# Eight-head attention layers: q and k in two rounded-fp32 parts, 48 rows per head, two heads in the two 64-row halves of the array

## The reference

```python
h = group_norm(x, 32 groups) * gn_w + gn_b
qkv = einsum('oc,bct->bot', qkv_w, h) + qkv_b          # 3 x 128 rows
q, k, v = split of qkv.reshape(B * 8, 3 * 16, T)
w = softmax(einsum('bct,bcs->bts', q * scale, k * scale))   # 1024 x 1024 per head
a = einsum('bts,bcs->bct', w, v)
x = x + einsum('oc,bot->bct', proj_w, a) + proj_b
```

## Time and profile before

| | |
|---|---|
| median of 3 runs | 2327.98 us (2327.2 to 2330.86) |
| profiled execution: span, first to last instruction | 2324.5 us |
| what lies around the span (median less span) | 3.5 us |
| TensorE busy / weight loads busy | 2210.8 us (95%) / 974.3 us |
| DVE busy / ACT busy / POOL busy | 1817.7 us / 1720.3 us / 520.4 us |
| mean granted TensorE clock | 0.987 |

### The profile page before, as it was taken

One profiled execution on the slowest core, in us unless ns is written; L12 is line 12 of the kernel. 1 busy time (PEld: TensorE's weight loads), 2 busy tenths in 40 slices (PEclk: granted clock), 3 DMA queues, 4 the chain that ended last, 5 costly groups with the idle time before them and its releaser, 6 DMA issues. The chain is left out here.

```text
span 2324.5 us, 34217 instructions
## 1 busy us (share of the span) xinstructions
PE 2210.8 (95%) x11776; PEld 974.3 (42%) x11776; DVE 1817.7 (78%) x3176; ACT 1720.3 (74%) x3107; POOL 520.4 (22%) x689
## 2 busy tenths in 40 slices
PE   3999999999999999999999999999998999999998
PEld 1223232323332232333233232323325888888887
DVE  2878878878887887888788878888846777777776
ACT  1467777767866776777777777777777888888887
POOL 3113030302213030212113030212003333333331
PEclk9999999999999999999999999999998999999999
DMA  8053361606243361616154251606102121121111
GB/s 153 10 66 58 52 79 44 94 20 91 44 65 60 51 89 25 100 26 88 34 77 62 47 79 33 105 22 91 25 16 75 43 67 57 42 66 57 42 52 48
DMA packets 81935, 136.86 MB, mean 59 GB/s; under 512 B 17760, under 2 KB 50656, under 8 KB 81632
## 3 DMA queue, kind: packets, MB, share of 16 engines
q1 hardware_dynamic: 78496, 133.90, 32.4%
q10 hardware_dynamic: 3264, 0.79, 0.2%
HBM read 57.31 MB, written 22.02 MB: 34 GB/s over the span
## 5 line engine op out<-in xcount | busy, mean ns | idle before, releaser
L450 DVE TENSOR_REDUCE h_half_nmax<-h_s_ps 128x1 f32<-128x512 f32 x2048 | 1286.8, 685 | 299.3 <-PE h_s_ps L689 292.3
L603 ACT ACTIVATE h_probs<-h_st_ps 128x512 f32<-128x512 f32 x2048 | 1104.2, 599 | 417.3 <-PE h_st_ps L826 411.4
L826 PE MATMUL h_st_ps<-h_qrep,h_krep 99*128 99x512 bf16 x2048 | 784.0, 384 | 54.1 <-issue 24.9
L689 PE MATMUL h_s_ps<-h_krep,h_qrep 96*128 96x512 bf16 x2048 | 799.6, 391 | 22.4 <-SPq L232 20.9
L681 PE MATMUL h_pv<-h_probs,h_vT 128*32 128x512 f32 x4096 | 552.0, 611 | 0.9 <-ACT h_probs L603 0.7
L689 PEld LDWEIGHTS h_s_ps<-h_krep,h_qrep 96*128 96x128 bf16 x2048 | 200.5, 98 | 682.4 <-DVE h_half_nmax L450 500.7
L826 PEld LDWEIGHTS h_st_ps<-h_qrep,h_krep 99*128 99x128 bf16 x2048 | 202.6, 99 | 251.5 <-issue 56.2
L1343 PE MATMUL o_s<-o_k,o_q 128*128 128x512 f32 x768 | 225.1, 429 | 7.4 <-DVE o_q L1164 5.7
L348 POOL TENSOR_SCALAR h_nparts<-h_nmax 128x16 bf16<-128x16 f32 x64 | 16.4, 256 | 956.0 <-DVE h_nmax L458 956.0
L1343 PE MATMUL o_pv<-o_pT,o_vT 128*128 128x512 f32 x768 | 207.3, 406 | 0.8 <-ACTq L1270 0.8
L1158 DVE TENSOR_TENSOR o_pT<-o_t,o_pT 128x512 fp32r<-128x512 f32 x256 | 164.6, 685 | 45.6 <-ACT o_pT L1295 43.1
(11 more groups left out here) (116 smaller groups left out, 1381.3 us busy)
## 6 DMA issues: line engine op xcount, KB each, us to landing
h_krep<-h_kp SPq DMA_DIRECT2D x96, 256.0 KB, 8.6
h_qrep<-h_qp SPq DMA_DIRECT2D x192, 128.0 KB, 9.5
x_res<-out_dram SPq DMA_DIRECT2D x32, 512.0 KB, 3.4
num<-av SPq DMA_DIRECT2D x128, 64.0 KB
rrep<-rden_dram SPq DMA_DIRECT2D x16, 512.0 KB
out_dram<-o_y SPq DMA_DIRECT2D x16, 512.0 KB
h_x_in<-out_dram SPq DMA_DIRECT2D x15, 512.0 KB, 3.4
out_dram<-h_y SPq DMA_DIRECT2D x15, 512.0 KB, 2.7
```

Of the source, the lines that this page charges most:

```text
L450: reduce = nc.vector.tensor_reduce(half_nmax[:, c, unit:unit + 1], s_ps[bank(2 * n + c)][:, :], AX.X, ALU.max, negate=True)
L603: nc.scalar.activation(probs[g % 2][:, j, :], st_ps[bank(n)][:, :], ACT.Exp, scale=1.0 / CH ** 0.5).then_inc(exp_done, 1)
L689: nc.tensor.matmul(s_ps[bank(n)][:, :], qrep[par][0:KS, th, head, tile * P:(tile + 1) * P], krep[par][0:KS, head, c * HALF:(c + 1) * HALF] ...
L826: nc.tensor.matmul(st_ps[bank(n)][:, :], krep[par][0:KM, head, st * P:(st + 1) * P], qrep[par][0:KM, th, head, :], start=True, stop=True). ...
```

## The change

q and k are split into two fp32r parts (a rounded one and what is left), and three products are kept: 3 x 16 = 48 rows of contraction per head, 51 with the maxima. Head 2m goes to rows 0 to 63 and head 2m+1 to rows 64 to 127, and their matmuls stand next to each other in TensorE's order. The maxima stay in three bf16 parts but travel as fp32r, in two DMAs. The rows of ones are filled at the start, before the coefficients, and `replicate` waits for them. TensorE's order in a group becomes st0, st1, s0, s1, st2, st3, products(k-1), s2, s3, shared bank.

```diff
-TERMS = 6
+TERMS = 3
+ROWS = P // 2
 KS = TERMS * CH
-KM = KS + 3
+MAX_PARTS = 3
+KM = KS + MAX_PARTS
...
-        qrep = [sb(f"qrep{i}", [P, 2, HEADS, HALF], BF16) for i in range(2)]
-        krep = [sb(f"krep{i}", [P, HEADS, T], BF16) for i in range(2)]
+        qrep = [sb(f"qrep{i}", [P, 2, HEADS // 2, HALF], F32R) for i in range(2)]
+        krep = [sb(f"krep{i}", [P, HEADS // 2, T], F32R) for i in range(2)]
...
         def split_parts(engine, own, which):
-            own.mark(tt(middle, whole, lead, ALU.subtract))
-            own.done(tt(rest[:, :], whole, lead, ALU.subtract))
-            own.done(tt(last, rest[:, :], middle, ALU.subtract))
+            own.done(engine.tensor_tensor(parts[which][:, 1, :], full[which][:, :], parts[which][:, 0, :].bitcast(F32),
+                                          ALU.subtract))
...
             def replicate(par, u):
-                for term, part in enumerate((0, 1, 2, 0, 1, 0)):
-                    sp.dma_start(krep[par][term * CH:(term + 1) * CH, :, :], parts["k"][:, part, :]).then_inc(rep_dma, 16)
+                for term, part in enumerate((0, 0, 1)):
+                    for r in range(2):
+                        to, of = r * ROWS + term * CH, slice(r * ROWS, (r + 1) * ROWS)
+                        sp.dma_start(krep[par][to:to + CH, :, :].bitcast(F32),
+                                     parts["k"][of, part, :].bitcast(F32)).then_inc(rep_dma, 16)
...
+                for term, part in enumerate((0, 1, 0)):
+                    for r in range(2):
+                        for th in range(2):
+                            sp.dma_start(qrep[par][to:to + CH, th, :, :].bitcast(F32), ...
...
+            sp.wait_ge(ones, 1)
             replicate(0, 0)
...
             pool.wait_ge(consts, CONSTS)
+            for par in range(2):
+                for r in range(2):
+                    own.done(nc.gpsimd.memset(krep[par][r * ROWS + 32:(r + 1) * ROWS, :, :].bitcast(F32), 1.0))
+            pool.sem_inc(ones, 1)
...
             def send_max_rows(step, th):
-                act.dma_start(qrep[par][KS:KM, th, quad * QUAD:(quad + 1) * QUAD, :],
-                              mrow[th][:, :]).then_inc(mrow_dma, 16)
+                for r in range(2):
+                    act.dma_start(qrep[par][r * ROWS + KS:r * ROWS + KM, th, quad * 2:(quad + 1) * 2, :].bitcast(F32),
+                                  mrow[th][r * MAX_PARTS * MP:(r + 1) * MAX_PARTS * MP, :].bitcast(F32)).then_inc(mrow_dma, 16)
...
+                    def scores_ahead(k, c):
+                        for r in range(2):
+                            n = STEP * s + 4 * k + 2 * c + r
+                            pe.wait_ge(max_done, last_in_bank(n) + 1 + 4)
+                            row_scores(n, ms // 2 % 2, ms % 2, pair, c, r)
+
+                    def column_scores(k, m):
+                        for r in range(2):
+                            n = QUAD * (GROUPS * s + k) + 2 * m + r
+                            rows = slice(r * ROWS, r * ROWS + KM)
+                            pe.wait_ge(exp_done, last_in_bank(n) + 1 + QUAD)
+                            nc.tensor.matmul(st_ps[bank(n)][:, :], krep[par][rows, quad * 2 + m, st * P:(st + 1) * P],
+                                             qrep[par][rows, th, quad * 2 + m, :],
+                                             start=True, stop=True).then_inc(st_ready, 1)
...
                     for k in range(GROUPS):
+                        column_scores(k, 0)
+                        scores_ahead(k, 0)
+                        column_scores(k, 1)
+                        if not (first and s == 0 and k == 0):
+                            products(k - 1)
+                        scores_ahead(k, 1)
+                        in_shared_bank(k)
```

More of the change, by code:

```diff
@@ L105, in many_heads @@
     MH = UNITS // 2
+    MP = MH // 2
     LEAD = 12
@@ L476, in _ @@
             dve.sem_inc(misc_for_dve, -3)
-            for unit in range(2 * LEAD):
-                maximum(unit - 2 * LEAD, unit, 2 * LEAD)
+            for pair in range(LEAD):
+                for c in range(2):
+                    maximum(4 * (pair - LEAD) + 2 * c, pair, c, 4 * LEAD)
             dve.sem_inc(scores_ready, -4 * LEAD)
@@ L505, in body @@
                                 output(base + 4, 0, no_output)
-                        for unit in (2 * k, 2 * k + 1):
-                            if s % 2 == 1 and unit % 2 == 1 and STATS <= k < STATS + 4 and not (last and s == 3):
+                        for c in range(2):
+                            if s % 2 == 1 and c == 1 and STATS <= k < STATS + 4 and not (last and s == 3):
                                 if k == STATS:
@@ L684, in group_products, with row_scores @@
                 return product
[L686 to L690, removed]
+            def row_scores(n, par, quad, pair, c, r):
+                th, m, tile = pair // MP, quad * 2 + pair % MP // (TILES // 2), pair % (TILES // 2)
+                rows = slice(r * ROWS, r * ROWS + KS)
+                nc.tensor.matmul(s_ps[bank(n)][:, :], qrep[par][rows, th, m, tile * P:(tile + 1) * P],
+                                 krep[par][rows, m, c * HALF:(c + 1) * HALF],
                                  start=True, stop=True).then_inc(scores_ready, 1)
@@ L805, in in_shared_bank @@
                                 project_output(1)
-                    def m_unit(unit, half):
-                        of_next, m = divmod(unit + 2 * LEAD, UNITS)
+                    def scores_ahead(k, c):
+                        of_next, pair = divmod(k + LEAD, GROUPS)
                         ms = s + of_next
@@ L811, in m_unit @@
                             return
-                        n = STEP * s + 2 * unit + half
-                        pe.wait_ge(max_done, last_in_bank(n) + 1 + 4)
-                        if m == 0 and half == 0 and ms % 2 == 0:
+                        if pair == 0 and c == 0 and ms % 2 == 0:
                             pe.wait_ge(rep_ready, u + 1)
-                        row_scores(n, ms // 2 % 2, ms % 2, m, half)
-                    for k in range(GROUPS):
[L819 to L828, removed]
-                            if j == 2 and not (first and n < QUAD):
-                                products(k - 1)
-                            m_unit(2 * k + j // 2, j % 2)
-                            if j == 3:
-                                in_shared_bank(k)
```

78 lines of the change are left out of this document (41 added, 37 removed).

## The result

The changed kernel takes 2505.98 us (median of 4 runs, 2493.26 to 2514.55), the kernel before 2327.59 us beside it. The ratio is 1.0765 (95% interval 1.0724 to 1.0806): 178 us slower. Slower was forecast, at 2387 us and with 2480 as the upper end, so the measured time lies above the range.

What follows compares the result with a forecast made beforehand. TensorE's stream bounded the eight-head layers, 2.84 us per plain group; after the change, bank waits would, at 2.86. 16 x (3.7 + 2.1 - 1.7) = +66, -7 at the start, gave 2387 us (+59), range 2300 to 2480.

Steps and rivals of the forecast that it cites:

- TensorE's stream was the bound: Eight-head layers before the change: scores follow one another without waits, 2.84 us per plain group, DVE's floor 0.4 below.
- a pair streams in the time of one: Scores of two heads in the two row halves: a pair takes 0.23 us, four pairs 0.92 instead of 1.75.
- The waits for banks become the chain.: Plain groups in the new order: s2, its reduction, s1, st3, products with three banks; 2.86 us per group, +0.02.
- Exposed four-byte loads, 0.16 a group.: Weight loads at s2 and s1 that cannot hide: 0.08 us each, twice in the chain, 2.70 becoming 2.86.
- Shared-bank groups, +0.4 and +0.2.: Groups with a projection: k and q 4.10 us against 3.70, values and output 3.93; four of each per image.
- Two DMAs for the maxima, +2.1.: Two issues in a row hold ACT 1.5 us before exp1: +2.1 us per image, bounds 0 and 3.0.
- Replicate shorter in four-byte elements.: Copying of k and q: same bytes in four-byte elements land sooner, q ending near 964 instead of 977.
- The stall at the step's start: Wait for the maxima's send behind the replicate, group 5.40 instead of 3.7 us: it goes, -1.7 us per image.
- Start, -7.: Before the first row score: ones delay coefficients 8.5 us, shorter split and DMAs save more; 45.6 against 53.1 us.
- rival (d): A TensorE idling a third of the time stays at 1.2 GHz: groups about 1.4 us longer, near 3000 us; chance 0.05.

Runs made afterwards that it cites:

- e3_same_half: The changed kernel with every score matmul in rows 0 to 63, odd heads left out and even ones computed twice: 3858.08 us, ratio 1.658.
- e1_order: The changed kernel with TensorE's old order within a group, halves, types and DMAs as changed: 2365.01 us, ratio 1.0179.
- e2_bf16: The changed kernel with two parts, maxima rows and replicas in bf16, third part of q and k left out: 2334.69 us, ratio 1.0031.
- e7_spread: The changed kernel with the maxima's two DMAs apart, the first behind exp0, the second behind exp2: 2581.43 us.
- e9_all: e5_hold_late with the column scores over all 64 rows of a half, as in e6_rows64: 2280.32 us, ratio 0.9799.
- e10_all_spread: e9_all with the maxima's two DMAs apart, as in e7_spread: 2252.84 us, ratio 0.9689.
- e5_hold_late: e1_order with q's second-half DMAs held until the next step's maxima rows land, and ones filled after the coefficients: 2330.11 us, ratio 0.9979.
- e8_before_48rows: The kernel before with bf16 score matmuls over 48 rows instead of 96 and 99, and a smaller exponential scale: 3715.24 us (one run).
- e6_rows64: The changed kernel with column scores over all 64 rows of a half, the added 13 rows zeros against ones: 2457.84 us, ratio 1.0569.
- e4_twice: The changed kernel with st0 and st1 issued twice into the same bank: 2550.26 us, ratio 1.0967.

## Why the prediction was wrong

The direction and the chain were right, the size was not: +178 us instead of +59. By its own steps:

- **TensorE's stream was the bound, and a pair streams in the time of one.** Right: both matmuls of a pair in 0.50; without the pairing a group is 1 us longer at the lower level (e3_same_half).
- **"The waits for banks become the chain."** Right, and shown twice: the timeline has each step of it, and the order alone (e1_order) brings 2.94 to 2.70 and the time down by 141 us. The size was forecast as 2.86: 0.10 instead of 0.08 for an exposed load, twice, and 0.04 in the rest. Over 17 plain groups that is 1.4 us per image.
- **Exposed four-byte loads, 0.16 a group.** Right in kind; e2_bf16 measures 0.23 with the shorter steps of bf16 in it. The Trainium skill ("TensorE: Matmul & The Clock Gate", "Weight-path perf modes — Fast Weight Load (FWL) and DoubleRow") gives Fast Weight Load no win for fp32. The traces agree for fp32r: 195 ns a load in the changed kernel, 94 in e2_bf16.
- **Shared-bank groups, +0.4 and +0.2.** Mis-sized: k and q groups are 4.24 (+0.54, forecast 4.10), values 4.11 to 4.18 (+0.4, forecast 3.93). Groups 13 and 14 of a first step, which hold the output projection, are 4.64 and 4.15. Together with the plain groups this makes an image 6.6 longer at the upper level, forecast 4.1. That is 40 of the missing 119 us, about half of it from the plain groups.
- **Two DMAs for the maxima, +2.1.** Not measured by itself. Spreading the two issues brought 0.4 us per image in the changed order (e7_spread) and 1.4 in the old one (e9_all to e10_all_spread). So in the changed order little of what these groups cost (3.12 and 3.61 in a second step against 2.94) is the second issue; the rest has other causes that no run separates.
- **Replicate shorter in four-byte elements.** Wrong. The row it rested on, 512 KB in 3.4 us, is a load from DRAM into 128 partitions; the replicate writes 16 partitions of SBUF from SBUF. Its rate is 112 GB/s after (40 to 45 us) and 113 before; k's DMAs land in 9.3 us, 8.6 before. It lasts 29.2 us from SP's first issue of k to the last landing in both kernels (921.81 to 950.97, before 947.88 to 977.12), so POOL's shorter split for q saves nothing, and k is issued no earlier in its step (22.7 us behind the step's first products, before 21.4). The stall at the step's start went all the same, but for another reason: the replicate ends 51.9 us into the step (before 50.6), and the next step's st0 now comes 57 us into it, before 49. e1_order, with shorter steps, has the stall back. That the stall would go came true by luck, not by the step that forecast it.
- **Start, -7.** Wrong in sign, +6, by the same step: the time of a DMA in four-byte elements. The 8.5 us behind the ones were right (coefficients at 17.27), and so was the shorter split (k's first issue is 6.2 later, q's at 35.47), but the DMA's saving was not there. From k's first issue to the first row score it is 29.6 us in both. Filling the ones late gets 6.4 back (e5_hold_late).
- **The clock, rival (d), chance 0.05.** This is the step that put the time out of range: 72 us, without which it would lie at some 2434, inside it. It was weighed as all or nothing, 3000 us or none, on the ground that the groups near the end kept 0.39 while waiting. Those have 99 rows. In the changed kernel the same groups fall to the lower level: products 4.12 us apart and 1.93 long, at a granted 0.50 (1894.60 to 1932.10). Most of the lost time lies behind the turns of the loop, which was the rival's own example; how long that stretch gets when TensorE has less to do was not asked. The rival's price per group was low too, 1.4 against 4.59 - 2.94 = 1.65. The shape of the matmul, not only the waiting, goes into it: e8_before_48rows never waits and never rises, e6_rows64 waits as much as the changed kernel and lies at the lower level for 93 us instead of 261, e4_twice for 122. That both count is shown (e4_twice adds nothing but matmuls in the time of a wait); how they combine is not, and the length of a single stretch differs from turn to turn and run to run (e5_hold_late's runs span 57 us).

## What to carry to other kernels

Halving TensorE's streaming time pays only while its order leaves each reader the time that it has now: with three banks, issue the scores so that no reader's full latency lies between the products and the next products. A kernel whose matmuls use fewer rows and wait more can lose its clock; look at the granted clock by stage and fill idle rows with zeros where the result allows it (48 and 50 us here for 13 rows). And a small transfer on the critical path wants the bulk transfer before it held back, which was worth 1.3% in the kernel before without any other edit.

## What the runs showed of the hardware

- Two 48-row fp32r matmuls in the two 64-row halves start together (within 0.01 us) and stream in the time of one: 0.50 for both behind a wait, next pair 0.34 later, then 0.23 a pair.
- A four-byte load of 128 columns that cannot hide costs 0.10 more than the bf16 one, twice per group here, also where the contraction is 48 rows: the first matmul takes 0.50 against 0.39 (e2_bf16).
- With 48-row score matmuls, one at a time and without waits, TensorE stayed at 1.2 GHz for over 3 ms while 98% busy (e3_same_half, e8_before_48rows); with 96 and 99 rows the order of e8_before_48rows ran at 2.4 GHz (384 ns a matmul against 628).
- After the same hole at a turn of the loop the level stayed down for 7 us with 96 and 99 rows, for 24 or 72 us with paired halves of 48 and 51, and for 14 to 17 us with 48 and 64 (e6_rows64).
- SBUF to SBUF DMAs into 16 partitions moved 112 to 117 GB/s whether in bf16 or in fp32 and whether rows were 1, 2 or 4 KB.
